# Graph attention and a mixture of experts on one Trainium2 core: the two masks of a quarter tile are built apart in the fused stage

## The chip, the cores and the metric

The kernel runs on one core of one Trainium2 chip. The metric is the device time of one execution in microseconds (us); lower is better. The engines are named as the profile names them: PE is TensorE's matmul and PEld its weight load, DVE is VectorE, ACT is ScalarE, POOL is GpSimd and SP is SyncE, which here only issues DMAs. Each engine works through its own queue of instructions in order, and the engines meet at semaphores.

## What is computed

The reference takes 12500 nodes of 256 features and 212500 edges (src, dst), sorted by dst, and applies four layers, each on a layer norm of its input and added to it:

```python
def _L0_gnn_ref(x, edge_index, W, a_src, a_dst):          # attention over edges, 8 heads of 32
    h = jnp.einsum('ni,hio->hno', x, W)
    attn_src = jnp.einsum('hno,ho->hn', h, a_src[..., 0])
    attn_dst = jnp.einsum('hno,ho->hn', h, a_dst[..., 0])
    edge_attn = jax.nn.leaky_relu(attn_src[:, src] + attn_dst[:, dst], negative_slope=0.2)
    edge_attn_exp = jnp.exp(edge_attn - jnp.max(edge_attn))
    attn_sum = jax.ops.segment_sum(edge_attn_exp.T, dst, num_segments=N)
    attn_norm = edge_attn_exp / (attn_sum[dst].T + 1e-10)
    weighted_h = attn_norm[..., None] * h[:, src]
    out = jax.ops.segment_sum(weighted_h.transpose(1, 0, 2), dst, num_segments=N)
    return out.reshape(N, H * F_OUT) + x

def _L0_ffn_ref(x, Wr, br, W1, ..., Wo, bo):               # 8 experts, all of them on every node
    w = jax.nn.softmax(feat @ Wr + br, axis=-1)
    h = jax.nn.relu(_bn(jnp.einsum('bfd,edh->bfeh', x, W1) + b1, g1, be1, m1, v1))
    h = jax.nn.relu(_bn(jnp.einsum('bfeh,ehk->bfek', h, W2) + b2, g2, be2, m2, v2))
    y = jnp.einsum('bfeh,ehd->bfed', h, Wo) + bo
    return jnp.einsum('bfed,fe->bfd', y, w)

x = x + _L0_gnn_ref(_layernorm(x), edge_index, ...)
x = x + _L0_ffn_ref(_layernorm(x)[None], ...)[0]
x = x + _L1_gnn_ref(_layernorm(x), edge_index, ...)        # mean over edges, one matrix, a norm
x = x + _L1_ffn_ref(_layernorm(x)[None], ...)[0]           # router, one expert a node
```

The change lies in the stage that computes the edge part of the first layer together with the second layer.

## The kernel before

The nodes are cut into 98 tiles of 128. For each tile, 18 columns of 128 edges are handled (an edge that belongs to no node of the tile matches nothing), in four quarters of 5, 4, 5 and 4 columns. Two tiles make a group, so there are 49 groups, and a group has eight steps e = 0 to 7. The fused stage (`attend_mix`) runs two pipelines side by side. In step e of group q, the attention pipeline handles one quarter of a tile of the group two further on, and the expert pipeline handles expert e for the 256 nodes of group q. `Slot(q, i)` is the quarter that belongs to step i of group q. Two neighbouring quarters have their dstb, ST, V and psE in two buffers (`side`, by the parity of i); S, the ring of gathered rows and the lists have a place for each quarter of a tile.

A quarter passes through these pieces of work:

- SP, `stage`: three DMAs bring the source nodes (`src`), the target nodes (`dst`) and the target nodes once more, spread over all partitions (`dstb`). It waits until the quarter four steps back has been weighted (V_ok) and until both masks of the quarter two steps back are built (S_ok).
- GpSimd, `gather`: for each of its 4 or 5 columns, an indirect DMA brings the rows of 128 source nodes into `ring` (L1257).
- VectorE, `build`: the node-side mask S (edges on the partitions, L1305) and the edge-side mask ST (nodes on the partitions, L1310). At the first quarter of a tile the node numbers are raised first (L1300). S waits for `summed`, since the matmuls of the same quarter one tile back read that place.
- TensorE, `hand_out`: ST times the target nodes' terms gives psE (L1524).
- VectorE, `weigh`: the factor f of each edge and head (L1325), its maximum (L1330), and the weighted rows V (L1333).
- TensorE, `sum_up`: S times V is added up in psum over the 18 columns (m_acc, L1537).

An expert passes through `layer1` on TensorE, `relu1` on ScalarE, `low_h1` on VectorE, `layer2`, `relu2`, `low_h2`, `layer3` (into m_psY) and `add` on VectorE. Products are made of a high and a low part each (`products_of`, L550; the low parts are `low_...` on VectorE, L538), so a layer of an expert is 12 matmuls of 256 columns.

The order on each engine is written out by hand. In step e VectorE does, in this order: build(e+2), low_h2(e-1), low_h1(e), weigh(e), then at some steps a piece of the layer norms, of the end of the attention (`attended`, `front_start`, `front_end`) or of the router's softmax, and add(e-1). TensorE does layer1(e+1), hand_out(e+1), layer3(e-1), at some steps a transpose or the router, layer2(e), and sum_up(e-1). At e = 0 TensorE does layer1 of experts 0 and 1, sum_up lies behind layer3, and VectorE has low_h1 behind add. The loop of the instruction streams holds two groups in one pass; one group lies ahead of the loop and four lie behind it. The first 16 quarters are handled ahead of the groups (`starts`), without experts, and the last two groups have no quarters left to build.

`at_least(eng, one, count)` is a wait that is left out while its count isn't positive, and `hold` increments a semaphore of bookkeeping that nobody waits for in this stage.

Of the kernel before, what the change touches and what calls it, by code (L numbers as in the profile page):

```python
# [17 lines left out]
P = 128  # L18
# [1077 lines left out]
def attend_mix(nc, a, k, scratch, ctx, sem, sbuf, psum):  # L1096
# [51 lines left out]
    def s_(name):  # L1148
# [4 lines left out]
    nodes_ok, S_ok, E_ok, f_ok, w_ok, V_ok, summed, U_ok = map(s_, (  # L1153
        "nodes_ok", "S_ok", "E_ok", "f_ok", "w_ok", "V_ok", "summed", "U_ok"))
# [27 lines left out]
    with nc.Block() as block:  # L1182
        @block.sync
        def _(sp):
            def stage(s):

                if not s.exists:
                    return
                at_least(sp, V_ok, s.a - 3)
                hold(sp, passed)  # L1190
                at_least(sp, S_ok, s.a * 2 - 2)
                hold(sp, passed)
                e0 = sp.value_load(k["visits"][0:1, bass.ds(s.n, 1)], min_val=0, max_val=ET * P)
                edges = bass.ds(e0 + s.first * P, s.size * P)
                for to, name in ((src, "src_p"), (dst, "dst_p")):
                    sp.dma_start(to[:, s.first:s.first + s.size], scratch[name][edges].rearrange("(p c) -> p c", c=s.size))\
                        .then_inc(staged[s.c], 16)
                sp.dma_start(dstb[s.side][:, 0:s.size * P], scratch["dst_p"][edges].rearrange("(x c) -> x c", x=1)
                             .to_broadcast([P, s.size * P])).then_inc(staged[s.c], 16)
# [85 lines left out]
        def _(v):  # L1285
# [6 lines left out]
            def build(s):  # L1292
# [3 lines left out]
                if s.c == 0:  # L1296
# [5 lines left out]
                v.wait_ge(staged[s.c], s.n * 48 + 48)  # L1302
                at_least(v, summed, s.a - 3)
# [6 lines left out]
                nc.vector.tensor_scalar(  # L1310
                    ST[s.side][:, 0:s.size, :], dstb[s.side][:, 0:s.size * P].rearrange("q (p c) -> q c p", c=s.size),
                    node_col[s.par][:, :], None, ALU.is_equal).then_inc(S_ok, 1)
# [144 lines left out]
            for i in range(2):  # L1457
                build(Slot(starts[0], i))
            for q in starts:
                for e in range(NX):  # L1460
# [12 lines left out]
                    build(Slot(q, e + 2))  # L1473

            def body(q, before, after):

                for e in range(NX):
                    build(Slot(q, e + 2))
# [5 lines left out]
                    weigh(Slot(q, e))  # L1484
                    if e == 0:
# [3 lines left out]
                        low_h1(q, 0)  # L1489
                        start_sum(q)  # L1490
# [24 lines left out]
        def _(pe):  # L1515
            def hand_out(s):
# [3 lines left out]
                pe.wait_ge(S_ok, s.a * 2 + 2)  # L1520
# [7 lines left out]
            def sum_up(s):  # L1528
# [3 lines left out]
                pe.wait_ge(V_ok, s.a + 1)  # L1532
                if s.c == 0:
# [949 lines left out]
```

## Time and profile before

| | us |
|---|---|
| median of 3 runs | 6864.84 (6863.64 to 6866.27) |
| the profiled execution | 6859.51 |
| its span | 6857.8 |
| TensorE busy in the span | 5382.0 (78%) |
| VectorE busy | 4435.0 (65%) |
| GpSimd busy | 4046.4 (59%) |
| ScalarE busy | 1813.6 (26%) |

The fused stage covers about half of the span. A row of a timeline gives the start, the duration, the engine, the line and the operation, out<-in, the shapes and how many were merged; in brackets stands the idle time of the engine just before it and what ended that. The ends of matmuls are modelled, and a wait that ends with an event that the profile doesn't show is put down to "issue". The durations of neighbouring VectorE instructions overlap by some 0.1 us, so intervals are taken from start to start.

### The profile page before, as it was taken

The page shows a single profiled execution, that of the slowest core. Times are in us where ns is not written, and L with a number is a line of the kernel's source. Part 1 is how long each engine was busy: PE and PEld are TensorE (multiplying, and loading weights), DVE is VectorE, ACT ScalarE, POOL GpSimd, SP SyncE. Part 2 cuts the span into 40 slices and gives each one's busy share as a digit, 9 for nine tenths or more (in the row PEclk, how much of TensorE's full clock was granted, in tenths as well). Part 3 has the DMA queues.
Part 4 walks back from the last instruction along what each step waited for, and adds up shares of the span by engine and source line. Part 5 has one row for each costly group of instructions (what it writes and reads, how often), then busy time and mean ns, then how long its engine had stood idle before and what let it go on. Part 6 is the DMA issues. An engine that isn't in the chain of part 4 may idle for free. (4 is left out here: it accounts for less than half of the span.)

```text
span 6857.8 us, 120850 instructions
## 1 busy us (share of the span) xinstructions
PE 5382.0 (78%) x32110; PEld 4807.6 (70%) x32111; DVE 4435.0 (65%) x11425; ACT 1813.6 (26%) x4248; POOL 4046.4 (59%) x4038
## 2 busy tenths in 40 slices
PE   4338999999999999999999566676676666675887
PEld 3338888888888888888888455555555555554887
DVE  6437878887888887878787344444544444444666
ACT  2203333333333333333333200000000000002554
POOL 1456666666666666666664277777777777772111
PEclk9659999999999999999999877777777777777999
DMA  6555455555454545555554144444444444443221
GB/s 200 126 165 141 133 141 133 141 133 140 133 142 132 143 132 141 134 139 136 137 137 119 56 126 127 127 126 128 127 123 122 121 117 119 117 116 106 76 77 47
DMA packets 655369, 863.49 MB, mean 126 GB/s; under 512 B 284046, under 2 KB 463712, under 8 KB 654322
## 3 DMA queue, kind: packets, MB, share of 16 engines
q0 software_dynamic: 183296, 501.40, 27.1%
q1 hardware_dynamic: 440572, 320.89, 16.7%
q10 hardware_dynamic: 31094, 35.88, 1.5%
q8 instruction: 244, 4.00, 0.2%
q14 instruction: 163, 1.34, 0.1%
HBM read 714.85 MB, written 155.09 MB: 127 GB/s over the span
## 5 line engine op out<-in xcount | busy, mean ns | idle before, releaser
L1257 POOL DMA_INDIRECT m_ring<-tab_a,m_src x1764 | 1964.3, 1114 | 1229.8 <-DMA m_dstb<-dst_p 710.3
L1848 POOL DMA_INDIRECT eb_rows<-tab_b,eb_src x1568 | 1492.6, 952 | 483.9 <-issue 476.2
L2019 PE MATMUL eb_acc<-eb_rows,eb_S 128*128 128x257 f32 x3528 | 1310.8, 533 | 497.0 <-DMA eb_rows<-tab_b,eb_src 481.1
L2019 PEld LDWEIGHTS eb_acc<-eb_rows,eb_S 128*128 128x128 f32 x3528 | 932.6, 279 | 731.1 <-issue 549.9
L1537 PE MATMUL m_acc<-m_V,m_S 128*128 128x264 f32 x3528 | 865.8, 392 | 0.0
L1537 PEld LDWEIGHTS m_acc<-m_V,m_S 128*128 128x128 f32 x3528 | 652.8, 193 | 93.0
L1651 ACT ACTIVATE mh_full<-m_ps,bn_b,bn_s 128x256 f32<-128x256 f32 x784 | 400.0, 560 | 1198.2 <-DVE mh_low L538 950.1
L538 DVE TENSOR_TENSOR mh_low<-mh_full,mh_high 128x512 fp32r<-128x512 f32 x784 | 542.3, 692 | 157.5 <-ACT mh_full L1662 144.1
L1662 ACT ACTIVATE mh_high<-m_ps,bn_b,bn_s 128x256 fp32r<-128x256 f32 x784 | 441.3, 563 | 705.9 <-PE m_ps L550 704.1
L1333 DVE TENSOR_TENSOR m_V<-m_ring,m_V 128x1280 f32<-128x1280 f32 (+1 forms) x392 | 532.6, 1359 | 57.5
L550 PE MATMUL m_psY<-mWo_low,mh_high 128*128 128x256 f32 x1568 | 351.2, 306 | 250.1 <-issue 238.3
L1305 DVE TENSOR_TENSOR m_S<-m_nodes,m_dst 128x640 f32<-128x640 f32 (+1 forms) x392 | 297.4, 759 | 345.4 <-PE m_acc L1537 282.0
L1524 PEld LDWEIGHTS m_psE<-q,m_ST 128*128 128x128 f32 x3528 | 436.4, 194 | 59.6 <-issue 55.0
L1524 PE MATMUL m_psE<-q,m_ST 128*128 (+1 forms) x3528 | 427.5, 256 | 50.7 <-DVE m_f L1325 31.7
L1662 ACT ACTIVATE mh_full<-m_ps,bn_b,bn_s 128x256 f32<-128x256 f32 x784 | 440.5, 562 | 0.0
L550 PEld LDWEIGHTS m_psY<-mWo_low,mh_high 128*128 128x128 f32 x1568 | 244.5, 194 | 275.4 <-issue 275.3
L1310 DVE TENSOR_SCALAR m_ST<-m_dstb,m_col 128x640 f32<-128x640 int32 (+1 forms) x392 | 402.5, 1027 | 0.0
L550 PE MATMUL m_ps<-mXT_low,mW_high 128*128 128x256 f32 x1568 | 375.5, 321 | 14.6 <-issue 14.1
L2246 POOL DMA_INDIRECT out_dram<-xYR,xtok x76 | 74.7, 983 | 516.6 <-DVE xYR L2299 505.0
L1446 DVE SCALAR_TENSOR_TENSOR macc<-m_psY,mwg,macc 128x256 f32<-128x256 f32 x784 | 340.9, 476 | 18.6 <-PE m_psY L550 18.1
L550 PE MATMUL m_ps<-mh_low,mW_high 128*128 128x256 f32 x1568 | 331.4, 294 | 1.6 <-issue 1.2
L550 PE MATMUL m_psY<-mWo_high,mh_high 128*128 128x256 f32 x1568 | 326.4, 291 | 0.0
(348 smaller groups left out, 10684.6 us busy)
## 6 DMA issues: line engine op xcount, KB each, us to landing
m_dstb<-dst_p SPq DMA_DIRECT2D x196, 320.0 KB
m_dstb<-dst_p SPq DMA_DIRECT2D x196, 256.0 KB
buf<-fill SPq DMA_DIRECT2D x49, 771.0 KB
m_ring<-tab_a,m_src POOLq DMA_INDIRECT x1764
eb_rows<-tab_b,eb_src POOLq DMA_INDIRECT x1568, 2.8
xw_stage<-in_L_ffn_w_dram ACTq DMA_DIRECT2D x16, 1024.0 KB, 8.2
over<-b_blank SPq DMA_DIRECT2D x9, 1452.0 KB, 15.4
mOV<-over SPq DMA_DIRECT2D x49, 264.0 KB
```

Source lines behind the costliest of these rows:

```text
L538: return nc.vector.tensor_tensor(low, full, high.bitcast(FP32), SUB)
L550: last = nc.tensor.matmul(out, x[i], y[j], start=n == 0, stop=n == len(steps) - 1)
L1257: gp.indirect_dma_start(out=ring[:, j, :], out_offset=None, in_=scratch["tab_a"], in_offset=bass.IndirectOffsetOnAxis(ap=src[:, j:j + 1], ...
L1310: nc.vector.tensor_scalar(ST[s.side][:, 0:s.size, :], dstb[s.side][:, 0:s.size * P].rearrange("q (p c) -> q c p", c=s.size), node_col[s.pa ...
L1333: nc.vector.tensor_tensor(to[:, 0:size, 0:D].rearrange("p t (h o) -> p t h o", h=H), got[:, :, 0:D].rearrange("p t (h o) -> p t h o", h=H) ...
L1446: nc.vector.scalar_tensor_tensor(acc[p][:, j, :], psY[:, j * D:(j + 1) * D], wg[p][:, j, e:e + 1], acc[p][:, j, :], MUL, ADD).then_inc(y_o ...
L1524: last_i = nc.tensor.matmul(psE[s.side][:, j * 16:j * 16 + 2 * H], ST[s.side][:, j, :], k["q"][:, bass.ds(s.n, 1), :].rearrange("p x c -> ...
L1537: last_i = nc.tensor.matmul(ps_acc[s.par][:, 0:NA], S[:, s.first + j, :], V[s.side][:, j, :], start=s.first + j == 0, stop=s.first + j == ...
L1651: ins = nc.scalar.activation(hf1[:, m, :], ps1[:, m * T2:(m + 1) * T2], ACT.Relu, bias=bn_b[0][:, c:c + 1], scale=bn_s[0][:, c:c + 1])
L1662: ins = nc.scalar.activation(part[:, m, :], ps2[:, m * T2:(m + 1) * T2], ACT.Relu, bias=bn_b[1][:, c:c + 1], scale=bn_s[1][:, c:c + 1])
L1848: gp.indirect_dma_start(out=rows_[par][:, to, 0:D], out_offset=None, in_=scratch["tab_b"], in_offset=bass.IndirectOffsetOnAxis(ap=index[:, ...
L2019: return nc.tensor.matmul(ps_acc[par][:, 0:NR], S[par][:, j, :], rows_[par][:, j, :], start=start, stop=False)
```

## The change

VectorE's `build` is split. `build_ST` raises the node numbers where a tile begins, waits for the staged lists and for E_ok, and builds the edge-side mask; it counts on a semaphore of its own, ST_ok. `build_S` waits for `summed` and builds the node-side mask. In a step of a group, build_ST stands first and build_S behind weigh; at e = 0 build_S stands behind low_h1 and ahead of start_sum. In the steps ahead of the groups the two follow each other, ST first. TensorE's hand_out waits for ST_ok instead of S_ok, and sum_up waits for S_ok behind V_ok. SP's stage waits for ST_ok instead of S_ok.

```diff
--- before.py
+++ after.py
@@ -1150,8 +1150,8 @@
     const = s_("const")
     staged = [s_(f"staged{c}") for c in range(4)]
     gathered = [sem(ctx, f"m_gathered{c}", pool_dma=True) for c in range(4)]
-    nodes_ok, S_ok, E_ok, f_ok, w_ok, V_ok, summed, U_ok = map(s_, (
-        "nodes_ok", "S_ok", "E_ok", "f_ok", "w_ok", "V_ok", "summed", "U_ok"))
+    nodes_ok, S_ok, ST_ok, E_ok, f_ok, w_ok, V_ok, summed, U_ok = map(s_, (
+        "nodes_ok", "S_ok", "ST_ok", "E_ok", "f_ok", "w_ok", "V_ok", "summed", "U_ok"))
     g_in = [s_(f"g_in{i}") for i in pair]
     g_free, over_ok, den_ok, rec_ok, att_ok, x1_ok = map(s_, ("g_free", "over_ok", "den_ok", "rec_ok", "att_ok", "x1_ok"))
     st_ok, mv_ok, ve_ok, rs_ok, xl_ok = map(s_, ("st_ok", "mv_ok", "ve_ok", "rs_ok", "xl_ok"))
@@ -1188,7 +1188,7 @@
                     return
                 at_least(sp, V_ok, s.a - 3)
                 hold(sp, passed)
-                at_least(sp, S_ok, s.a * 2 - 2)
+                at_least(sp, ST_ok, s.a - 1)
                 hold(sp, passed)
                 e0 = sp.value_load(k["visits"][0:1, bass.ds(s.n, 1)], min_val=0, max_val=ET * P)
                 edges = bass.ds(e0 + s.first * P, s.size * P)
@@ -1289,7 +1289,7 @@
             for par in pair:
                 nc.vector.tensor_scalar(node_col[par][:, :], col_i[:, :], float((par - 2) * P), None, ADD).then_inc(nodes_ok, 1)
 
-            def build(s):
+            def build_ST(s):
 
                 if not s.exists:
                     return
@@ -1300,6 +1300,16 @@
                         nc.vector.tensor_scalar(x[s.par][:, :], x[s.par][:, :], float(2 * P), None, ADD).then_inc(nodes_ok, 1)
                     v.wait_ge(nodes_ok, s.n * 2 + 6)
                 v.wait_ge(staged[s.c], s.n * 48 + 48)
+                at_least(v, E_ok, s.a - 1)
+                hold(v, passed)
+                nc.vector.tensor_scalar(
+                    ST[s.side][:, 0:s.size, :], dstb[s.side][:, 0:s.size * P].rearrange("q (p c) -> q c p", c=s.size),
+                    node_col[s.par][:, :], None, ALU.is_equal).then_inc(ST_ok, 1)
+
+            def build_S(s):
+
+                if not s.exists:
+                    return
                 at_least(v, summed, s.a - 3)
                 hold(v, passed)
                 nc.vector.tensor_tensor(
@@ -1307,9 +1317,6 @@
                     node_no[s.par][:, :].rearrange("p (x n) -> p x n", x=1).to_broadcast([P, s.size, P]),
                     dst[:, s.first:s.first + s.size].rearrange("p (t y) -> p t y", y=1).to_broadcast([P, s.size, P]),
                     ALU.is_equal).then_inc(S_ok, 1)
-                nc.vector.tensor_scalar(
-                    ST[s.side][:, 0:s.size, :], dstb[s.side][:, 0:s.size * P].rearrange("q (p c) -> q c p", c=s.size),
-                    node_col[s.par][:, :], None, ALU.is_equal).then_inc(S_ok, 1)
 
             def weigh(s):
 
@@ -1455,7 +1462,8 @@
                 normed(acc[q.par], XL2, count, 1)
 
             for i in range(2):
-                build(Slot(starts[0], i))
+                build_ST(Slot(starts[0], i))
+                build_S(Slot(starts[0], i))
             for q in starts:
                 for e in range(NX):
                     weigh(Slot(q, e))
@@ -1470,23 +1478,27 @@
                             softmax_start(g0)
                         if e == 4:
                             softmax_end(g0)
-                    build(Slot(q, e + 2))
+                    build_ST(Slot(q, e + 2))
+                    build_S(Slot(q, e + 2))
 
             def body(q, before, after):
 
                 for e in range(NX):
-                    build(Slot(q, e + 2))
+                    build_ST(Slot(q, e + 2))
                     if e:
                         low_h2(q, e - 1)
                         low_h1(q, e)
                     elif before:
                         low_h2(q.prev(), NX - 1)
                     weigh(Slot(q, e))
+                    if e:
+                        build_S(Slot(q, e + 2))
                     if e == 0:
                         if before:
                             add(q.prev(), NX - 1)
                             back_start(q.prev(), q.n * 2 + 1)
                         low_h1(q, 0)
+                        build_S(Slot(q, e + 2))
                         start_sum(q)
                     if e == 1 and before:
                         back_end(q.prev(), q.n * 2 + 1)
@@ -1517,7 +1529,7 @@
 
                 if not s.exists:
                     return
-                pe.wait_ge(S_ok, s.a * 2 + 2)
+                pe.wait_ge(ST_ok, s.a + 1)
                 at_least(pe, f_ok, s.a - 1)
                 hold(pe, passed)
                 for j in range(s.size):
@@ -1530,6 +1542,8 @@
                 if not s.exists:
                     return
                 pe.wait_ge(V_ok, s.a + 1)
+                hold(pe, passed)
+                pe.wait_ge(S_ok, s.a + 1)
                 if s.c == 0:
                     at_least(pe, U_ok, s.n - 1)
                 hold(pe, passed)
```

## Rows read from the trace of the kernel before

**Rows 1.** Stretches: us, then busy us of PE, PEld, DVE, ACT, POOL; PEclk, DMA, GB/s.

```profile
613.00:3758.00 3145.00, 2912.53 (x20738) 2739.83 (x20737) 2528.65 (x5018) 1177.26 (x2489) 1932.15 (x1830) 0.98 0.51 136
```

**Rows 2.** Groups by line, PE, 613 to 3758: busy us, mean ns | idle before.

```profile
L550 PE MATMUL m_psY<-mWo_low,mh_high 128*128 128x256 f32 x1476 | 331.0, 306 | 217.9 <-issue 206.6 <-DVE mh_low L538 11.3
```

**Rows 3.** Timeline, PE, one group, the stalls of layer 3.

```profile
2275.68 0.47 PE L550 MATMUL m_psY<-mWo_low,mh_high 128*128 128x256 f32 x2 [0.74 <-issue]
2283.53 0.48 PE L550 MATMUL m_psY<-mWo_low,mh_high 128*128 128x256 f32 x2 [0.54 <-issue]
2291.81 0.47 PE L550 MATMUL m_psY<-mWo_low,mh_high 128*128 128x256 f32 x2 [0.74 <-issue]
...
2307.71 0.47 PE L550 MATMUL m_psY<-mWo_low,mh_high 128*128 128x256 f32 x2 [0.76 <-issue]
2315.58 0.48 PE L550 MATMUL m_psY<-mWo_low,mh_high 128*128 128x256 f32 x2 [1.09 <-issue]
2323.85 0.36 PE L550 MATMUL m_psY<-mWo_low,mh_high 128*128 128x256 f32 x1 [0.52 <-issue]
```

**Rows 4.** Timeline, DVE, the same group, e=1 to 4.

```profile
2266.62 0.69 DVE L538 TENSOR_TENSOR mh_low<-mh_full,mh_high 128x512 fp32r<-128x512 f32 x1 [2.18 <-ACT mh_full L1662]
...
2272.87 0.82 DVE L1305 TENSOR_TENSOR m_S<-m_nodes,m_dst 128x640 f32<-128x640 f32 x1 [0.88 <-PE m_acc L1537]
2273.61 1.37 DVE L1310 TENSOR_SCALAR m_ST<-m_dstb,m_col 128x640 f32<-128x640 int32 x1
2274.90 0.68 DVE L538 TENSOR_TENSOR mh_low<-mh_full,mh_high 128x512 fp32r<-128x512 f32 x1
...
2281.56 0.69 DVE L1305 TENSOR_TENSOR m_S<-m_nodes,m_dst 128x512 f32<-128x512 f32 x1
2282.16 0.67 DVE L1310 TENSOR_SCALAR m_ST<-m_dstb,m_col 128x512 f32<-128x512 int32 x1
2282.76 0.68 DVE L538 TENSOR_TENSOR mh_low<-mh_full,mh_high 128x512 fp32r<-128x512 f32 x1
...
2291.03 0.68 DVE L538 TENSOR_TENSOR mh_low<-mh_full,mh_high 128x512 fp32r<-128x512 f32 x1
```

**Rows 5.** Timeline, ACT, the last activation ahead of low_h2(6).

```profile
2313.20 0.57 ACT L1662 ACTIVATE mh_full<-m_ps,bn_b,bn_s 128x256 f32<-128x256 f32 x1
```

**Rows 6.** Timeline, DVE, e=7 and a turn of the loop.

```profile
1562.98 0.68 DVE L538 TENSOR_TENSOR mh_low<-mh_full,mh_high 128x512 fp32r<-128x512 f32 x1
...
1565.38 1.23 DVE L1333 TENSOR_TENSOR m_V<-m_ring,m_V 128x1024 f32<-128x1024 f32 x1
...
1571.24 0.83 DVE L1305 TENSOR_TENSOR m_S<-m_nodes,m_dst 128x640 f32<-128x640 f32 x1 [3.30 <-issue]
```

**Rows 7.** Timeline, PE, the same turn of the loop.

```profile
1563.76 0.47 PE L550 MATMUL m_psY<-mWo_low,mh_high 128*128 128x256 f32 x2 [1.09 <-issue]
...
1570.16 0.48 PE L550 MATMUL m_ps<-mXT_low,mW_high 128*128 128x256 f32 x2 [1.09 <-issue]
...
1574.09 0.48 PE L550 MATMUL m_psY<-mWo_low,mh_high 128*128 128x256 f32 x2 [1.24 <-DVE mh_low L538]
```

**Rows 8.** Timeline, PE, e=7 and e=0 inside a pass.

```profile
1357.96 0.47 PE L550 MATMUL m_psY<-mWo_low,mh_high 128*128 128x256 f32 x2 [1.09 <-issue]
1367.76 0.47 PE L550 MATMUL m_psY<-mWo_low,mh_high 128*128 128x256 f32 x2 [0.54 <-issue]
```

**Rows 9.** Stretch behind 1357.96, columns as in rows 1.

```profile
1358.00:1360.00 2.00, 2.00 (x13) 2.00 (x14) 1.64 (x5) 0.00 (x0) 0.09 (x1) 0.70 0.97 268
```

**Rows 10.** Timeline, DVE, V at e=3.

```profile
2285.14 1.22 DVE L1333 TENSOR_TENSOR m_V<-m_ring,m_V 128x1024 f32<-128x1024 f32 x1
```

**Rows 11.** Timeline, POOL, the first gathers of the quarter staged then.

```profile
2296.08 1.08 POOL L1257 DMA_INDIRECT m_ring<-tab_a,m_src  x1 [2.42 <-issue]
2297.46 0.95 POOL L1257 DMA_INDIRECT m_ring<-tab_a,m_src  x1 [0.30 <-issue]
```

**Rows 12.** Groups by line, POOL, 613 to 3758.

```profile
L1257 POOL DMA_INDIRECT m_ring<-tab_a,m_src x1644 | 1832.1, 1114 | 1177.3 <-DMA m_dstb<-dst_p 698.9 <-issue 464.7 <-DVE mmv L1363 13.7
```

## The prediction

> **What bounds the kernel now.** I read the stretches first. The fused stage, in its steady part, fills 3145 of the 6857.8 us, with TensorE busy for 2912.53 us at a mean granted clock of 0.98, and VectorE busy for 2528.65 us [rows 1]. TensorE sets the pace there, and what it loses is idle time. The groups by line say where: 217.9 us of it stand ahead of one kind of matmul, the first of layer 3 (into m_psY) [rows 2]. The timeline of one group shows that stall at e=2, 3, 4, 6, 7 and at e=0 of the next group: 0.74, 0.54, 0.74, 0.76, 1.09 and 0.52 us, together 4.39 us, and none at e=5 [rows 3]. From e=7 to e=7 three groups take 1563.76 - 1357.96 = 205.8 us, 68.6 us each [rows 7, 8].
>
> Layer 3 of expert e-1 waits for low_h2(e-1). Why is that late? The timeline of VectorE at e=2 shows it: VectorE has run out of work and sits idle for 0.88 us, up to 2272.87, until TensorE ends sum_up (m_acc). Then come the node-side mask S (0.74 us to the next start), the edge-side mask ST (1.29 us) and, at 2274.90, low_h2 [rows 4]; layer 3 begins at 2275.68 [rows 3]. So the tail of TensorE's own step, plus two masks, lies ahead of the operand for which TensorE waits next. S is held because its quarter of the buffer is read by that sum_up; ST isn't, but stands behind S in the queue.
>
> **What the change does to a step.** No arithmetic goes or comes: both masks keep their form. Per quarter VectorE gains one wait (ST on E_ok) and one semaphore increment; TensorE gains one wait and one increment before sum_up. Behind VectorE's new wait stand low_h2, low_h1 and the weighted rows. E_ok counts hand_out(e), which TensorE did a whole step earlier, so I take the wait at 0. For the wait and the increment themselves the nearest rows are S(512) to ST(512), 0.60 us with none between, and ST(512) to low_h2, 0.60 us with both [rows 4]: 0 by the rows. From above I allow 0.05 us, an estimate at about the reading error of such gaps, which on 376 quarters would be 19 us; a gain from them has no reason. TensorE's second wait is on a mask built over two steps before: 0 too. SP's staging is still released by the weighted rows V, its second wait having been met before; the three small transfers and their order on SP are unchanged, and GpSimd's queue is untouched. S's wait for sum_up(e-2) moves behind V(e), when that sum has long been over: the stall in front of S goes. S also stands ahead of add(e-1) and, at e=0, of start_sum; add(e-1) frees psY for layer 3 of expert e, but low_h2(e), still further back in VectorE's queue, holds that anyway.
>
> **Step by step.** All starts here are of rows 4, but for layer 3, whose starts are of rows 3. At e=1 low_h2(0) starts at 2266.62, after 2.18 us of idle time that ScalarE ends. Nothing on VectorE holds it, so that start stays and is the anchor.
> - e=2: VectorE is next free at 2272.87 - 0.88 = 2271.99. S (512 wide, 0.60) now lies ahead of that. From the node numbers to ST there is a dependence that the wait for sum_up hid; no row shows it, so it lies between 0 and the 0.88 that hid it, and I take 0.2, near the lower end, since the operations are small. Then ST, 1.29: low_h2(1) starts at 2274.08 instead of 2274.90. TensorE would want layer 3 at 2275.68 - 0.74 = 2274.94; from the start of low_h2 to layer 3 it is 0.78 us, so 2274.86. The 0.74 us go, with 0.08 to spare.
> - e=3: VectorE doesn't idle from 2274.90 to 2282.76. The interval of 7.86 us gets 0.14 longer (S of 640 instead of 512): low_h2(2) at 2282.08, layer 3 at 2282.85 instead of 2283.53. What is saved since the anchor falls from 0.74 to 0.68.
> - e=4: 8.27 us, again without idling, less 0.14: low_h2(3) at 2290.21, layer 3 at 2291.00 instead of 2291.81, saved 0.81. VectorE itself is the bound at e=3 and 4, and about 0.6 us of stall is left at each.
> - e=5: no stall before, none after. e=6: the 0.76 us go, VectorE having caught up.
> - e=7: low_h2(6) is then released by ScalarE, whose last activation started at 2313.20 and took 0.57 [rows 5]. In the old times low_h2 could start at 2313.80 and layer 3 at 2314.58, against the 2315.58 - 1.09 = 2314.49 wanted: of 1.09 I book 1.00.
>
> Sum of e=2 to 7: 0.81 + 0.76 + 1.00 = 2.57 us a group.
>
> e=0 has two forms. Inside a loop pass (two groups) the stall is 0.52 and goes: low_h2(7) isn't held by sum_up any longer. At the turn of the loop VectorE starts S only after 3.30 us that no wait explains [rows 6], TensorE itself pauses 1.09, and layer 3 then stalls for 1.24; from layer 3 at e=7 to the next it is 1574.09 - 1563.76 = 10.33 us [rows 7], against 2323.85 - 2315.58 = 8.27 inside [rows 3]. VectorE's pause moves with its queue. New, from low_h2(6): 1565.38 - 1562.98 = 2.40 to V(7), 2.56 for V, add and softmax_end (up to 1571.24 - 3.30), 0.60 for S, 3.30 pause, 1.29 ST = 10.15 [rows 4, 6]. I book 0.18.
>
> **Clock.** Behind the 1.09 us stall of e=7 at 1357.96 the granted clock of the next stretch is 0.70, so it fell to the lower level (1.2 GHz) inside it [rows 9]. Short stretches from 1000 to 2900 us show 18 such falls in 28 groups, every one at that place; rows 9 hold one. At a turn of the loop they cost nothing that I see. Inside a pass layer 3 to layer 3 is then 1367.76 - 1357.96 = 9.80 instead of 8.27 [rows 8, 3]: 1.53 us, in 6 of 14, so 0.66 for an e=0 inside a pass. With the stall gone I count them gone; the bounds are 0 and 0.66. The Trainium skill, "TensorE: Matmul & The Clock Gate", section "HAM oscillation — how this bites in real kernels", blames idle gaps longer than any here; by it the falls would be no matter of this stall and could stay, for 15 us less gain.
>
> **Sum.** 46.5 of the 49 groups have masks to build: 46.5 x 2.57 = 120 us. 23 turns x 0.18 = 4, 23 inside x (0.52 + 0.66) = 27. Together 151 us. The profiled execution took 6859.5 us, 1.7 above its span, so 6708.5; the median of the runs is 5.3 above it: 6714.
>
> **Rivals.**
> 1. The falls of the clock don't go but move, to the turns of the loop, where TensorE would idle about 1.1 + 1.1 us close together: 15 us not gained, plus 23 x 1.53 = 35 us. That gives 6764. For it: they follow idle time. Against: 1.09 + 1.24 us at a turn already stand in rows 7, and the falls lie elsewhere.
> 2. Staging becomes ST's wait. V(3) began at 2285.14 and took 1.22 [rows 10]; the gather that needs the same transfers resumed at 2296.08, 9.7 us after its end [rows 11]. The new ST(7) is due some 10.7 us after V(3), so 1.0 us is left. A landing 2 us later would cost 1 to 1.5 us a group, 47 to 70 us: 6761 to 6784. Against: S and ST wait for the same landing today, and what held S is TensorE.
> 3. The other side: gathering becomes the bound. GpSimd does 36 gathers a group, of 1832.1 / 1644 = 1.114 us [rows 12] and with 0.30 between two [rows 11]: 51 us, with the two norms about 53, of 68.6. A denser VectorE could stretch them. GpSimd binds from a mean of 1.44 us, and the kernel is slower than before from 1.54. At 1.6 the group takes 70.7, 2.1 x 46.5 = 98 us more: 6963. Single gathers took 0.95 us, so some are far above the mean. The Trainium skill, "SBUF — State Buffer", section "SBUF: two separate sides", has GpSimd and VectorE take one port pair by an exclusive lock, whoever starts first; rows 11 and 12 agree as far as they go. But VectorE's work isn't more, only closer, so the mean should rise by a few per cent.
> 4. The stall isn't VectorE's queue: ScalarE's results are late everywhere as at e=1, and nothing moves: 6865. Against: 0.88 us of idle time ahead of S, none ahead of low_h2(1) [rows 4].
> 5. Better: VectorE's 3.30 us pause runs while it would be idle anyway. Then up to 1.24 us more at each of 23 turns, 28 us: 6686.
>
> **Chances.** Forecast 0.59 (6695 to 6740 by itself), rival 1 0.13, rival 2 0.09, rival 3 0.04, rival 4 0.06, rival 5 0.09. The range is 6675 to 6780. A measurement of this kernel tells 0.2%, 14 us, from no change. Faster 0.90, same 0.06, slower 0.04.
>
> **What would show it.** Right: ST starting behind add, before sum_up has ended; no idle time ahead of S; stalls of layer 3 of 0, 0.6, 0.6, 0, 0 and 0.1 us at e=2 to 7 and, at e=0, 0 inside and above 1 at a turn; psY's idle total at 80 to 110 us; a clock of 0.99 or 1.00. Wrong: ST waiting for m_dstb; idle time before m_f on m_ring; falls of the clock behind a turn; stalls at e=3 and 4 above 0.6, which would mean that VectorE binds harder than I reckon.

## The result and the profile after

The changed kernel takes 6743.99 us (median; 6741.79 to 6754.14) against 6865.56 us for the kernel before on the same chip: a ratio of 0.9825, 95% interval 0.9814 to 0.9837. That is 121.6 us less, where the forecast had 151. The profiled execution has a span of 6741.8 us.

The same stage, which ends earlier now, answers to [rows 1]; columns as there.

```profile
613.00:3640.00 3027.00, 2883.08 (x20743) 2712.40 (x20742) 2533.52 (x5014) 1180.79 (x2493) 1959.87 (x1830) 0.99 0.54 141
```

The stage is 118 us shorter. TensorE is busy for 29 us less in it (the same matmuls, more of them at the full clock), and VectorE for as long as before. The groups by line of PE in that stretch, answering to [rows 2], and with them the first matmul of layer 1:

```profile
L550 PE MATMUL m_ps<-mXT_low,mW_high 128*128 128x256 f32 x1480 | 358.2, 324 | 45.3 <-issue 45.3
L550 PE MATMUL m_psY<-mWo_low,mh_high 128*128 128x256 f32 x1476 | 327.7, 304 | 98.6 <-issue 84.6 <-DVE mh_low L538 6.2
```

The idle time ahead of layer 3 fell from 217.9 to 98.6 us, inside the 80 to 110 foretold. But 45.3 us now stand ahead of layer 1, where the kernel before has 14.1.

The timeline of VectorE at e=1 to 4 of one group, answering to [rows 4]:

```profile
1344.15 0.69 DVE L538 TENSOR_TENSOR mh_low<-mh_full,mh_high 128x512 fp32r<-128x512 f32 x1 [2.04 <-ACT mh_full L1676]
...
1347.76 0.68 DVE L1315 TENSOR_TENSOR m_S<-m_nodes,m_dst 128x512 f32<-128x512 f32 x1
...
1349.93 0.14 DVE L1300 TENSOR_SCALAR m_col<-m_col 128x1 f32<-128x1 f32 x1
1350.40 1.43 DVE L1305 TENSOR_SCALAR m_ST<-m_dstb,m_col 128x640 f32<-128x640 int32 x1 [0.33 <-DVE m_col L1300]
1351.75 0.67 DVE L538 TENSOR_TENSOR mh_low<-mh_full,mh_high 128x512 fp32r<-128x512 f32 x1
...
1359.15 0.67 DVE L1305 TENSOR_SCALAR m_ST<-m_dstb,m_col 128x512 f32<-128x512 int32 x1
1359.74 0.69 DVE L538 TENSOR_TENSOR mh_low<-mh_full,mh_high 128x512 fp32r<-128x512 f32 x1
...
1368.08 0.68 DVE L538 TENSOR_TENSOR mh_low<-mh_full,mh_high 128x512 fp32r<-128x512 f32 x1
```

The node-side mask S stands behind the weighted rows, with nothing idle ahead of it. ST starts behind the node numbers, and low_h2(1) comes 7.60 us behind low_h2(0), where it was 8.28. At e=6 ST runs beside TensorE's sum_up, which it no longer waits for; the two rows are of PE and of DVE:

```profile
1379.40 2.39 PE L1551 MATMUL m_acc<-m_V,m_S 128*128 128x264 f32 x10
1380.21 1.40 DVE L1305 TENSOR_SCALAR m_ST<-m_dstb,m_col 128x640 f32<-128x640 int32 x1 [0.33 <-DMA m_dstb<-dst_p]
```

Over the groups from 1000 to 3300 us ST starts 1.55 us ahead of sum_up's end at e=6 and 1.15 us ahead of it at e=7. At e=2 to 5 VectorE comes to ST only 0.16 to 1.78 us behind that end (means of each step). So what e=2 gains is not that ST is free, but that S no longer stands there.

The stalls of layer 3 on PE in the group that starts at 1344 us, answering to [rows 3], are at e=1, 3 and 4; e=2, 5, 6, 7 and the next e=0 have none:

```profile
1344.94 0.47 PE L550 MATMUL m_psY<-mWo_low,mh_high 128*128 128x256 f32 x2 [0.33 <-issue]
1360.53 0.47 PE L550 MATMUL m_psY<-mWo_low,mh_high 128*128 128x256 f32 x2 [0.69 <-issue]
1368.87 0.48 PE L550 MATMUL m_psY<-mWo_low,mh_high 128*128 128x256 f32 x2 [0.81 <-issue]
```

The list of VectorE's waits (engine, line, releaser: us in total, times, longest) had the wait for TensorE's sum_up at its head in the kernel before, here from 613 to 3600 us:

```profile
DVE m_S L1305 <- PE m_acc L1537: 265.7, 169, 3.5
```

After, from 613 to 3640 us, it has no wait for m_acc any more, and next to none for the staged numbers:

```profile
DVE mh_low L538 <- ACT mh_full L1676: 136.7, 95, 2.9
...
DVE m_ST L1305 <- issue: 73.5, 39, 3.7
DVE macc L1453 <- PE m_psY L550: 35.1, 36, 3.1
...
DVE m_ST L1305 <- DMA m_dstb<-dst_p: 1.3, 3, 0.6
```

GpSimd's gathers, answering to [rows 12], took 1127 ns each, 13 more than before:

```profile
L1257 POOL DMA_INDIRECT m_ring<-tab_a,m_src x1644 | 1853.1, 1127 | 1022.1 <-DMA m_dstb<-dst_p 540.1 <-issue 469.8 <-DVE mmv L1370 12.2
```

**Where the missing 30 us are.** I took the start of layer 3 of every expert from 1000 to 3300 us (34 to 36 groups) and averaged the eight intervals of a group. Where one interval spans the turn of the loop it is put apart. In us:

```
                    e1-e2 e2-e3 e3-e4 e4-e5 e5-e6 e6-e7   e7-e0 in / turn   next e0-e1   mean group
before               8.27  7.86  8.29  7.16  8.73  7.87     8.90 / 10.38       10.44        68.24
after                7.60  8.02  8.30  7.15  7.83  6.89     7.59 / 11.17       10.87        65.79
```

"Next e0-e1" is that behind a turn. Inside the pass the forecast holds: 2.39 us go from e=1 to e=7 (2.57 reckoned) and 1.31 at e7-e0 (1.18). At the turn, where 0.18 should have gone, 0.79 came, and 0.43 behind it: 22 turns x (0.18 + 0.79 + 0.43) = 31 us. (The prediction reckoned with 23 turns; the loop has 22 passes.)

The timelines of one turn, PE and then DVE, answering to [rows 7] and [rows 6]:

```profile
1127.68 2.39 PE L1551 MATMUL m_acc<-m_V,m_S 128*128 128x264 f32 x10
1133.01 0.47 PE L550 MATMUL m_ps<-mXT_low,mW_high 128*128 128x256 f32 x2 [2.94 <-issue]
```

```profile
1129.30 0.17 DVE L1431 TENSOR_TENSOR mwg<-mlg,mls 128x16 f32<-128x16 f32 x1
1133.18 1.39 DVE L1305 TENSOR_SCALAR m_ST<-m_dstb,m_col 128x640 f32<-128x640 int32 x1 [3.71 <-issue]
...
1140.44 0.87 DVE L1453 SCALAR_TENSOR_TENSOR macc<-m_psY,mwg,macc 128x256 f32<-128x256 f32 x2 [3.05 <-PE m_psY L550]
```

VectorE's pause is the old one, a few tenths longer. TensorE's is new in size: 2.94 us, with no wait that would explain it, where it was 1.09. The stretches behind it, columns as in [rows 1]:

```profile
1130.00:1132.00 2.00, 0.07 (x1) 0.00 (x0) 0.00 (x0) 0.00 (x0) 1.70 (x2) 1.00 0.55 115
1132.00:1134.00 2.00, 0.99 (x6) 1.02 (x7) 0.82 (x1) 0.00 (x0) 1.10 (x2) 0.88 0.52 150
1134.00:1136.00 2.00, 2.00 (x12) 1.85 (x11) 1.61 (x5) 0.35 (x1) 0.00 (x0) 0.50 0.62 177
1136.00:1138.00 2.00, 2.00 (x10) 2.00 (x11) 1.39 (x1) 0.91 (x3) 0.00 (x0) 0.50 0.01 2
1138.00:1140.00 2.00, 2.00 (x12) 2.00 (x11) 0.00 (x0) 0.00 (x0) 1.22 (x2) 0.50 0.04 1
1140.00:1142.00 2.00, 2.00 (x9) 1.47 (x8) 1.41 (x4) 0.00 (x0) 1.61 (x2) 0.92 0.92 197
```

The granted clock falls to the lower level (0.50, that is 1.2 GHz) for some 7 us, and add then waits 3.05 us for a slow psY. From 1000 to 2800 us the clock falls 6 times, at 14 turns, every time behind such a pause (2.1 to 2.94 us); not every such pause brings a fall (one of 2.85 us brought none). The falls behind e=7 of the kernel before, 17 in that stretch, are gone.

It is the falls that cost, and not the pauses by themselves. Of the 17 turns from 1000 to 3300 us, 9 have a fall. There the interval e7-e0 and the next one take 23.29 us together. At the 8 turns without a fall they take 20.71, against 20.82 in the kernel before, though TensorE's pause at these 8 is 1.05 to 2.85 us long. So a fall costs 2.6 us here, and 22 turns x 9/17 x 2.6 = 30 us, which is all but 1 us of what the turns lack.

### The profile page after: what moved, and what is told of

Its sections match the earlier page's. It is cut to its first block and busy times, and to the rows that moved or that the text cites. A ratio compares the mean times of both kernels' runs of the same rounds, so it can differ in the third digit from the quotient of the medians.

```text
span 6741.8 us, 121635 instructions
## 1 busy us (share of the span) xinstructions
PE 5321.4 (79%) x32110; PEld 4747.4 (70%) x32111; DVE 4439.6 (66%) x11425; ACT 1816.6 (27%) x4248; POOL 4080.8 (61%) x4038
## 5 line engine op out<-in xcount | busy, mean ns | idle before, releaser
L2033 PE MATMUL eb_acc<-eb_rows,eb_S 128*128 128x257 f32 x3528 | 1275.9, 521 | 527.2 <-DMA eb_rows<-tab_b,eb_src 513.3
L2033 PEld LDWEIGHTS eb_acc<-eb_rows,eb_S 128*128 128x128 f32 x3528 | 902.6, 270 | 762.4 <-issue 592.3
L550 PE MATMUL m_ps<-mXT_low,mW_high 128*128 128x256 f32 x1568 | 377.4, 322 | 45.3 <-issue 45.3
L550 PEld LDWEIGHTS m_ps<-mXT_low,mW_high 128*128 128x128 f32 x1568 | 260.6, 191 | 90.6 <-issue 69.6
```

The lines of the kernel that those rows point to most:

```text
L550: last = nc.tensor.matmul(out, x[i], y[j], start=n == 0, stop=n == len(steps) - 1)
L2033: return nc.tensor.matmul(ps_acc[par][:, 0:NR], S[par][:, j, :], rows_[par][:, j, :], start=start, stop=False)
```

## The experiments

There are two questions: did the gain come from where the prediction had it, and why did TensorE's pause at the turn grow? "Turn" below is the interval e7-e0 there; the pause is TensorE's total ahead of layer 1 from 613 to 3600 us. All times are medians, and each ratio is to the kernel before, which is at 6865 to 6867 us in every comparison.

**1. The new semaphores with the old order.** From the kernel after:

```diff
-                    build_ST(Slot(q, e + 2))
+                    build_S(Slot(q, e + 2))
+                    build_ST(Slot(q, e + 2))
...
                     weigh(Slot(q, e))
-                    if e:
-                        build_S(Slot(q, e + 2))
...
                         low_h1(q, 0)
-                        build_S(Slot(q, e + 2))
```

The raising of the node numbers and the wait for the staged lists move with it, to build_S, which is the first of the two here; in the steps ahead of the groups S comes first too.

> The separate semaphores and the two extra waits alone, with the masks in their old places (S, then ST, both at the head of the step). If waits and increments cost nothing, as I booked them, the time is that of the kernel before, 6865 us, within 7. If each costs about 0.05 us on VectorE's or TensorE's path, it is 6885.

6862.66 us, ratio 0.9999 (0.9989 to 1.0009). The waits and increments by themselves cost nothing in the time here, and all of the gain is the order. Yet the trace isn't that of the kernel before: the pause is 29.2 us in place of 14.1, and the turn 10.83 in place of 10.38. Intervals inside the pass got shorter by as much (8.46 against 8.90, with 14 falls of the clock from 1000 to 2800 us against 17), so the sum hid it.

**2. Both masks early, ST ahead of S.**

```diff
                     build_ST(Slot(q, e + 2))
+                    build_S(Slot(q, e + 2))
...
                     weigh(Slot(q, e))
-                    if e:
-                        build_S(Slot(q, e + 2))
...
                         low_h1(q, 0)
-                        build_S(Slot(q, e + 2))
```

> Both masks stay at the head of the step, but ST goes ahead of S. S still waits for sum_up ahead of low_h2. Theory: what counts is that ST (1.29 us) no longer stands behind the wait for sum_up, and VectorE uses the idle time for it; S of 0.74 then still lets low_h2 go in time. By the steps of the prediction the low_h2 of e=2 moves by 0.15 us against the changed kernel and the one of e=4 by 0.14: 6750 to 6760 us. Rival: S itself ahead of low_h2 is what costs, and the place behind weigh is needed: 6800 us or more, with idle time left in front of S and stalls of layer 3 at e=6 and 7.

6790.56 us, 0.9893 (0.9876 to 0.9909): between the two kernels, and between the 6750 to 6760 of the theory and the 6800 of the rival. ST's 1.3 us now cover most of TensorE's tail, but S still waits for it:

```profile
DVE m_S L1315 <- PE m_acc L1549: 57.4, 85, 1.2
```

So three fifths of the gain (74 of 122 us) come with ST ahead of S, and the other 47 us with S behind the weighted rows. I had under-reckoned the second. About half of it lies in the steps: e=1 to 7 are longer by 0.51 us a group than in the change, 24 us, of which e6-e7 has 0.42 (7.31 against 6.89). Another 18 us lie at the turns, which take 11.80 us and the interval behind them 11.08, with pauses of TensorE of 55.8 us in total and 11 falls of the clock from 1000 to 2800 us.

**3. Both masks behind the weighted rows.**

```diff
                 for e in range(NX):
-                    build_ST(Slot(q, e + 2))
...
                     if e:
+                        build_ST(Slot(q, e + 2))
                         build_S(Slot(q, e + 2))
                     if e == 0:
+                        build_ST(Slot(q, e + 2))
```

> Both masks behind weigh (at e=0 ST behind weigh, S behind low_h1). Theory: from low_h2(0) to low_h2(3) VectorE is the bound, and this takes one wide ST (1.29 us) out of that stretch for a narrow one (0.60), so the stall at e=4 falls from 0.8 to 0.1 us, the one at e=3 stays at 0.7; at a turn of the loop the ST behind the 3.3 us pause goes, and with it the stall of layer 3 of about 1.1 us. 46 x 0.7 + 23 x 1.1 = 57 us less than the changed kernel: 6690 us. Rival: the stalls at e=3 and 4 have another bound, or ST comes too late for hand_out or for the staging behind it: 6744 or more, with TensorE idle ahead of m_psE or ST waiting for m_dstb.

6750.72 us, 0.9833 (0.9816 to 0.9849), no better than the change, where 6690 had been expected. e3-e4 fell as foretold, from 8.30 to some 7.6, but e4-e5 rose by 0.26 us and e6-e7 by 0.30, and the turn and what follows took 12.01 and 11.25 us: the pause is 62.4 us in total, and from 1000 to 3300 us 14 of 17 turns have a fall of the clock, where the change has 9.

**4. Work for TensorE's pause.** 16 matmuls at the end of a pass, with a result that nobody reads:

```diff
+                    if e == NX - 1 and not isinstance(q.n, int) and q.par == 0:
+                        for x in range(16):
+                            nc.tensor.matmul(ps1[:, 0:T2], W1.at(0, 0, slice(0, P))[0], XT[q.par].at(0)[0], start=True, stop=True)
```

> The changed kernel with 16 matmuls whose result nobody reads (1.9 us) at the end of each pass of the loop on TensorE. Theory: the pause of TensorE at a turn (1.05 to 2.94 us in the changed kernel) is a delay that runs from the moment when its sequencer meets the branch, so matmuls still queued cover it: the pause shrinks by up to 1.9 us, the turn gets no longer, and the falls of the clock behind it go, which are what the changed kernel lacks to the forecast: 6715 us. Rival: the pause starts only when the queue is empty. Then each turn gets 1.9 us longer, 22 x 1.9 = 42 us, with the falls gone or not: 6755 to 6785.

6780.04 us, 0.9877 (0.9861 to 0.9894), so 36 us slower than the change: the rival. Matmuls ahead of the pause didn't shorten it (50.3 us in total, up to 3.6, against 45.3), as if it began only when TensorE's queue is through. They are also instructions more in TensorE's pass, which may lengthen the pause by itself (experiment 5); this run doesn't tell the two apart.

**5. One semaphore for both masks.** The masks end alternately, so one count tells both; TensorE's second wait before sum_up goes, and with it the increment of bookkeeping (`hold`) beside it: 16 of each in a pass.

```diff
-                at_least(sp, ST_ok, s.a - 1)
+                at_least(sp, S_ok, s.a * 2 - 3)
...
-                    node_col[s.par][:, :], None, ALU.is_equal).then_inc(ST_ok, 1)
+                    node_col[s.par][:, :], None, ALU.is_equal).then_inc(S_ok, 1)
...
-                pe.wait_ge(ST_ok, s.a + 1)
+                pe.wait_ge(S_ok, s.a * 2 + 1)
...
                 pe.wait_ge(V_ok, s.a + 1)
-                hold(pe, passed)
-                pe.wait_ge(S_ok, s.a + 1)
```

> The masks in the places of the kernel after, but both counted on one semaphore as in the kernel before (the masks of a quarter end alternately, so the first one's count is odd and the second one's even). TensorE's sum of a quarter then has no second wait, and no instruction more stands in TensorE's loop than before the change. Theory (the two instructions more per quarter in TensorE's queue are what made the turn of the loop dearer: in split_only, with the old order and the new waits, the step at the turn took 10.83 us against 10.38): the step at the turn falls by about 0.45 us, 23 x 0.45 = 10 us, 6734 us or a little less, TensorE's pause ahead of the first m_ps of a pass falls from 2 to 3 us towards 1.1. Rival (the turn is dearer because TensorE reaches it with nothing queued, whatever the count of its instructions): 6740 to 6748, pauses as in the kernel after.

6719.33 us, 0.9788 (0.9771 to 0.9804), 25 us below the change, where the theory had 10; its interval doesn't touch the change's. Its list of PE's waits:

```profile
PE m_psY L550 <- issue: 83.8, 141, 0.9
PE m_ps L550 <- issue: 24.6, 21, 1.8
PE m_psY L550 <- DVE mh_low L538: 21.6, 20, 1.5
```

The pause fell to 0.9 to 1.8 us at each turn (from 45.3 to 24.6 in total), the turn to 10.23 us, the falls of the clock from 6 to 3. Turns without a fall take 20.61 us here with the interval behind them, against the change's 20.71: the gain, too, is for the most part falls that don't come, 4 at 17 turns in place of 9.

The wait that went had nothing to wait for: S is built over two steps before the V that TensorE awaits first. So what costs is that the wait and its increment stand in the queue; how they lengthen the pause is open. I looked at the transfers of instructions in the view of DMAs, queue q8, from 700 to 3600 us (packets, MB, share), in the kernel before, after, experiment 1 and this one:

```profile
q8 instruction: 201, 3.29, 0.5%
```

```profile
q8 instruction: 217, 3.56, 0.6%
```

```profile
q8 instruction: 212, 3.47, 0.5%
```

```profile
q8 instruction: 199, 3.26, 0.5%
```

The kernels with the extra wait fetch 11 to 18 packets more in these 21 to 22 passes, about one in a pass. But the size of the pause doesn't follow the packets: the kernel of experiment 9 has 199 of them and pauses for 29.9 us, where the kernel before has 201 and pauses for 14.1, and that of experiment 3 has 213 and pauses longest of all. And no row ties a packet to an engine. That the extra fetch is the pause isn't shown.

The four falls tell something more. One of them, in the rows of PE and the stretch below (columns as in [rows 1]), comes behind a pause of 0.93 us and a stall of 1.44 us for low_h2, a few us apart:

```profile
1129.32 0.48 PE L550 MATMUL m_ps<-mXT_low,mW_high 128*128 128x256 f32 x2 [0.93 <-issue]
1133.44 0.48 PE L550 MATMUL m_psY<-mWo_low,mh_high 128*128 128x256 f32 x2 [1.44 <-DVE mh_low L538]
```

```profile
1134.00:1136.00 2.00, 2.00 (x13) 1.79 (x12) 1.96 (x3) 0.00 (x0) 0.90 (x1) 0.70 0.00 0
```

Two more look the same (0.93 and 1.44, 1.07 and 1.18 us). That is about as much idle time as at the turn of [rows 7], 1.09 and 1.24 us, which had no fall.

**6 and 7. Four groups in a pass,** of the change and of the kernel before: 11 turns in place of 22, the same work.

```diff
-        with eng.Fori(0, (Q - 5) // 2) as i:
-            body(Group(i * 2 + 1, i, 1), True, True)
-            body(Group(i * 2 + 2, i + 1, 0), True, True)
+        with eng.Fori(0, (Q - 5) // 4) as i:
+            body(Group(i * 4 + 1, i * 2, 1), True, True)
+            body(Group(i * 4 + 2, i * 2 + 1, 0), True, True)
+            body(Group(i * 4 + 3, i * 2 + 1, 1), True, True)
+            body(Group(i * 4 + 4, i * 2 + 2, 0), True, True)
```

> The kernel after with four groups in a pass of the loop in place of two, so 11 turns in place of 22; all work and its order are the same. Theory (the gain that is missing went into the turn of the loop: two groups with a turn take 64.23 + 67.44 = 131.67 us, two with the seam inside a pass 2 x 63.82 = 127.64): each turn that goes gives back 4.0 us, 11 x 4.0 = 44 us, 6700 us. Rival (what costs is the fetching of instructions, which goes on with the length of the code and not with the branch: the pauses come as often, wherever they fall): 6735 to 6750, with pauses of 1 to 3 us ahead of m_ps or m_psY inside a pass.

> The kernel before with four groups in a pass, 11 turns fewer. Theory (the turn is cheap there: groups ending at a turn 69.02 us against 67.52 inside a pass): 11 x 1.5 = 17 us less, 6848 us, so the change is worth 6848 - 6700 = 148 us there, against 151 in the prediction's sum. Rival: the turn costs the same in both kernels (4 us), 6821, and the change is worth no more than the 122 us measured.

With the change it takes 6693.43 us, 0.9749 (0.9732 to 0.9765): 51 us below two groups in a pass, 7 more than foretold. Without it, 6862.21 us, 0.9994 (0.9985 to 1.0004), nothing, where I had expected 17 less: there the falls of the clock behind e=7 stay and even get more, 20 against 17, which the price of a turn had left out. So the change is worth 122 us with 22 turns and 169 with 11. The turn is the whole shortfall and more. The pauses come at turns only (9 from 1000 to 3300 us, in place of 18), though instructions are fetched all along (188 packets in q8 against 217, and 216 in q14 against 114): the pause hangs on the turn, not on the fetching as such.

**8 and 9. A cheaper mask.** The groups by line, by form, show what ST costs in the change with five columns and with four:

```profile
L1305 DVE TENSOR_SCALAR m_ST<-m_dstb,m_col 128x640 f32<-128x640 int32 x182 | 255.0, 1401 | 104.8 <-issue 73.5 <-DVE m_col L1300 28.5 <-DMA m_dstb<-dst_p 1.3
L1305 DVE TENSOR_SCALAR m_ST<-m_dstb,m_col 128x512 f32<-128x512 int32 x183 | 125.3, 685 | 17.8 <-DVE macc L1440 16.1
```

ST reads the edge numbers in steps of its count of columns. The edit has it read them in order and write in steps, first in the change and then in the kernel before. (The expectations call ST the node-side mask; it is the edge-side one, and the edit touches ST alone.)

```diff
-                    ST[s.side][:, 0:s.size, :], dstb[s.side][:, 0:s.size * P].rearrange("q (p c) -> q c p", c=s.size),
+                    ST[s.side][:, 0:s.size, :].rearrange("q c p -> q p c"),
+                    dstb[s.side][:, 0:s.size * P].rearrange("q (p c) -> q p c", c=s.size),
```

> The kernel after with the edge numbers read in the order in which they lie and the node-side mask written across (same numbers, same place). The mask of five columns takes 1.40 us and that of four 0.67 in the kernel after. Theory (the stepped read of five columns is what is slow): five columns take 0.7 to 0.85 us, VectorE's step with them is shorter by 0.6 us, the stalls of TensorE at the fourth and fifth products of a group (0.69 and 0.81 us) go for the most part, up to 46 x 1.2 = 55 us: 6690 to 6715. Rival (a stepped write costs what the stepped read does, or the width of five does): the mask takes 1.4 us or more at five columns, time 6744 or above.

> The kernel before with the node-side mask read in order and written across, nothing else. It tells what the same cheaper mask is worth where both masks stand ahead of the casts. Theory (the mask stands between one cast and the next in every step, so all of its 0.46 us at five columns is on the path in the even steps; 4 x 46.5 x 0.46 = 86 us less 4 x 46.5 x 0.10 = 18 us for the dearer four columns): about 68 us less, 6798 us, range 6780 to 6815. Rival (the kernel after is bound elsewhere too and got 90 us because it took the mask off the path only in part; before gains as much or more): 6775 or below.

The same two groups in the first of these kernels:

```profile
L1305 DVE TENSOR_SCALAR m_ST<-m_dstb,m_col 128x640 f32<-128x640 int32 x182 | 171.0, 940 | 106.0 <-issue 74.9 <-DVE m_col L1300 28.9 <-DMA m_dstb<-dst_p 1.2
L1305 DVE TENSOR_SCALAR m_ST<-m_dstb,m_col 128x512 f32<-128x512 int32 x183 | 143.0, 781 | 17.8 <-DVE macc L1441 16.1
```

With the change it takes 6653.35 us, 0.9687 (0.967 to 0.9703), 91 us less and more than the 55 of the theory (its profiled execution, 6676.9, lies at the upper end of its runs, so its trace shows only 65). Five columns take 0.94 us in place of 1.40, four 0.78 in place of 0.69. e3-e4 fell from 8.30 to 7.73, e2-e3 from 8.02 to 7.66, e1-e2 from 7.60 to 7.38: 1.15 us a group, 54 us, which is what the theory had counted. The mean group fell by 1.33; what the medians show beyond that no row of the trace explains. In the kernel before the edit gives 6770.48 us, 0.986 (0.9843 to 0.9876), 96 us less where 68 were expected; the rival had put the time at 6775 or below, and it came true. There e1-e2, e3-e4 and e5-e6 fell by 0.55 us each, the dearer four columns, booked at 18 us, don't show (e2-e3 7.83 for 7.86), and of 17 falls of the clock 8 remain. The change is worth 117 us on top of the cheaper mask: the two gains are separate. In the kernel before, S still waits for TensorE with the cheaper mask. The idle time ahead of its five-column form is about what it was, as the groups by form show, without the cheaper mask (613 to 3758 us) and with it (613 to 3600 us):

```profile
L1305 DVE TENSOR_TENSOR m_S<-m_nodes,m_dst 128x640 f32<-128x640 f32 x183 | 151.3, 827 | 260.8 <-PE m_acc L1537 243.2 <-issue 17.6
```

```profile
L1305 DVE TENSOR_TENSOR m_S<-m_nodes,m_dst 128x640 f32<-128x640 f32 x181 | 149.8, 828 | 256.0 <-PE m_acc L1538 188.6 <-issue 67.4
```

**10 to 12. Together.** The edits are those above: one semaphore (5) and the cheaper mask (8) in kernel 10; with four groups in a pass (6) in kernel 11; with both masks behind the weighted rows (3) too in kernel 12.

> one_sem and st_in_order together: masks as in the kernel after, one semaphore for both, the node-side mask read in order. Theory (two separate terms: a dearer turn of the loop, 25 us by one_sem, and the stepped read of five columns, 90 us by st_in_order): they add up, 6744 - 25 - 90 = 6629 us, or down to 6615, since st_in_order's pauses at the turn (up to 3.2 us) hold clock falls that one_sem took away. Rival (st_in_order's 90 us already hold what one_sem gives): 6650 or above.

> one_sem_in_order with four groups in a pass of the loop. Theory (a turn still costs 66.5 - 63.8 = 2.7 us in one_sem, and the falls behind some of them): 11 turns fewer take 11 x 2.7 to 3.0 = 30 to 33 us more, 6585 to 6600 us. Rival (once the extra waits are out of TensorE's queue a turn costs what it cost before the change, where four groups in a pass brought 4 us): 6625.

> best_four with both masks built behind the weighted rows (as in both_behind). Theory (both_behind lost its gain to TensorE's longer pauses at the turn and to the clock falls behind them; with half the turns, one semaphore and the cheaper mask that loss is gone, and no mask at all stands ahead of a cast): 6560 to 6590 us, below best_four. Rival (the edge products that follow the mask then come late, e4 to e5 and e6 to e7 are longer by 0.3 to 0.5 us as in both_behind): the same as best_four or up to 20 us above it.

Kernel 10 took 6644.27 us, 0.9678 (0.9662 to 0.9694); kernel 11 took 6621.96, 0.9648 (0.9631 to 0.9664); kernel 12 took 6607.75, 0.9628 (0.9612 to 0.9644). None reached its theory (6615 to 6629, 6585 to 6600 and 6560 to 6590 us). By the medians the single semaphore gives 9 us more on top of the cheaper mask, by the traces 25 (a mean group of 63.91 us against 64.46); the intervals don't decide between the two. Eleven turns fewer gave 22 us, between the 4 of the rival and the 30 of the theory: in kernel 11 the clock doesn't fall once from 1000 to 2800 us. In kernel 12 the losses of experiment 3 inside the pass are gone (e4-e5 7.15, e6-e7 6.90) and e3-e4 is 7.42. That the cheaper mask gives VectorE the slack for it is likely; no run here parts it from the other two edits. It is the fastest, 3.7% below the kernel before and 136 us below the change.

## Why the prediction was right, and where it fell short

- **The mechanism** (S waits for TensorE's tail and ST waits behind S): right. Idle time ahead of S is 0, and experiment 1 shows that the order is all of the gain. ST starting before sum_up has ended, a sign that the prediction named, came at e=6 and 7 only; at e=2 to 4 VectorE comes to ST later than that, and what e=2 gains is that S stands elsewhere.
- **e=2 to 7:** 2.39 us measured, 2.57 reckoned. e=6 and 7 gave 0.90 and 0.98 where 0.76 and 1.00 stood. e=2 to 4 gave 0.50 together, where 0.81 stood, so the sum is nearer than its terms. The wait behind the node numbers is 0.33 us, not 0.2, and the step of e=4 takes 8.34 us, not 8.13. The stall at e=4 is 0.8 us, not 0.6: VectorE binds there harder than I reckoned, as the text had as a sign. It is 8 us of the sum. Experiment 8 shows that the five-column mask could give back 0.46 us there.
- **e=0 inside a pass:** 1.31 against 1.18. The stall is gone, and so are the falls of the clock that followed e=7.
- **e=0 at a turn:** this step failed. I reckoned 10.15 us on VectorE's side and booked a gain of 0.18; it took 11.17, and 0.43 more behind it. The sum for VectorE wasn't wrong: with one semaphore the turn takes 10.23, and in the change the turns without a fall of the clock take 10.27. What failed is the price put on TensorE's second wait, "0 too", and the bound of 0.05 us a quarter (19 us), argued from gaps between VectorE's instructions. The cost, 25 us, lies on TensorE and not at the wait: at the turn, where the pause grows (14.1 us in total before, 45.3 in the change) and brings falls of the clock. Without a fall a turn is no dearer than before (20.71 against 20.82 us with the interval behind it); with one it costs 2.6 us more. In the old order nearly two thirds of that pause are there (29.2 of 45.3 us), and the time is that of the kernel before: the turns are dearer (10.83 against 10.38), and fewer falls behind e=7 make up for it.
- **Rival 1** (the falls move to the turns) came in part, and it is where the shortfall lies: falls at 9 of 17 turns, where it had one at each; by their cost, 30 us, where it had 35. I had argued against it that 1.09 + 1.24 us of idle time at a turn do no harm. That held at that turn, but it was no safe rule: the pauses grew beyond it, and in experiment 5 falls came behind 0.93 + 1.44 and 1.07 + 1.18 us as well. Inside a pass the falls are gone, so its other 15 us were gained.
- **Rival 2** (staging): 1.3 us of waiting in all. **Rival 3** (gathering): out; 1127 ns a gather against 1114, far from the 1440 at which it would bind. **Rival 4** (nothing moves): out. **Rival 5** (VectorE's pause hidden): out; ST waits 73.5 us for it, about 3.3 us at each of 22 turns.
- **The size:** 22 turns x 1.40 us = 31 and 8 at e=2 to 7, less 3 at e=0 inside a pass, make 36 us that the trace lacks; 30 by the medians. The range of 6675 to 6780 held the time.

The Trainium skill, "TensorE: Matmul & The Clock Gate", section "HAM oscillation — how this bites in real kernels", blames longer idle gaps for falls than the 1.09 us of the kernel before. Here the trace differs: with that stall gone, the falls behind it went. Falls in the change, from 1000 to 3300 us, follow pauses of 2.10 to 3.32 us.

## What to carry to other kernels

Where one wait guards two pieces of work, ask which of them needs it, and put the one that doesn't ahead; the wait of the other is then hidden behind work that has to be done anyway. Count the instructions that a change adds to the queue of the busiest engine, waits that never wait among them: look at the pause at the turn of its loop and at the clock behind it, and let one semaphore count two things if their order is fixed. When a turn gets dearer, part the turns with a fall of the clock from those without before blaming the pause. Price each form of an operation by itself: one mask of five columns cost twice that of four, and reading it in order was worth as much as three quarters of the whole change.

## What the runs showed of the hardware

- At the turn of a loop an engine pauses with no wait in the profile: VectorE about 3.3 us; TensorE 0 to 2.18 us in the kernel before, and 1.05 to 3.32 us with sixteen more waits and sixteen more increments in a pass. 16 matmuls ahead of it didn't shorten it (experiment 4), and with half the turns there are half as many pauses (experiment 6).
- TensorE's pauses of 1.05 to 2.85 us at a turn cost nothing that can be measured where the clock stayed up: these turns took 10.27 us, near the 10.15 reckoned for VectorE's work. A fall of the clock behind such a pause cost 2.6 us; by the stretches it lasts some 3 to 7 us at half rate.
- No length of pause parts falls from none: in the change pauses of 2.85 and 3.07 us brought none, and in experiment 5 a pause of 0.93 us with a stall of 1.44 us behind it did.
- A 32-bit integer operand read in steps of 5 elements made a VectorE comparison of 640 columns take 1401 ns, against 685 for 512 in steps of 4. Read in order and written in steps they take 940 and 781 ns. I hadn't expected the step of 5 to cost double that of 4.
